# One copy in four of an attention's turned weights on VectorE instead of ScalarE, and one blank matmul fewer ahead of each pair of units

## The chip, the cores and the metric

The kernel runs on one core of a Trainium2 chip. The metric is the device time of one execution in microseconds (us), the median of several runs. The core has four compute engines that run side by side, each of them through its own instructions in order: TensorE (PE in the profile; its weight loads are PEld), VectorE (DVE), ScalarE (ACT) and GpSimd (POOL). They wait for one another through semaphores.

## The reference, cut to what matters

The reference chains six layers on an input of 2 x 16 x 16 x 64. The change touches the first, a neighbourhood attention with 8 heads over windows of 7 x 7:

```
attn = einsum('bijnd,bijnpqd->bijnpq', q, kn) + bias        # kn: the 7 x 7 window of keys
a = softmax(attn.reshape(B, H, W, NH, K * K), axis=-1)
out = einsum('bijnpq,bijnpqd->bijnd', a, vn).reshape(B, H, W, C)
out = out @ proj_w + proj_b
gate = sigmoid(relu(x @ g1_w + g1_b) @ g2_w + g2_b)
y = x + out * gate                                           # then a layer norm
```

After it come a global attention, a dilated attention, a mixture of experts, a causal attention over the batch, and a recurrence over 256 positions (`h_new = o * tanh(c_new)`), each of them with a norm ahead of it and each needing the whole of the one before.

## The kernel before, in words

The first attention is cut into 16 units (`NU`). A unit is one batch element, one half of the 256 positions (128 rows) and one pair of heads; the window is handled as 176 dense keys with a bias of -1e30 outside it. Two units make a pair `s` that shares one set of score matmuls. For a unit `u` the work goes round the engines:

1. TensorE, `scores(s)` (L436): 8 matmuls for both units of a pair, into two banks. It waits for the row minima of the pair before the last (`neg_max`), then issues two blank matmuls (`keep_clock`, L394) from the third pair on. A blank matmul multiplies a tile of zeros into a free bank; nobody reads it.
2. VectorE, `row_min(u)` (L753): adds the bias and takes the row minimum, once per head.
3. ScalarE, `numerators(u)` (L275): the exponentials of both heads with their sums.
4. VectorE, `normalise(u)` (L760 and L762): reciprocal of the sums, then a multiplication per head in place.
5. TensorE, `turn(u)` (L448): four transposes into bank 4 or 5, by the parity of `u`. It waits for `normalise(u)` and for the copy of unit `u - 2`, whose bank it takes.
6. ScalarE, `turned_copy(u)` (L283): copies that bank, 88 partitions by 512 columns, to one of four tiles `pt`.
7. TensorE, `values(s)` (L463): 16 matmuls for a pair, which read the copies of both of its units.

The loops fix the order on each engine by hand. TensorE at an even step `u` issues `scores(u/2)`, `turn(u-3)`, `values(u/2-3)`, and at an odd step `turn(u-3)` alone. ScalarE at step `u` issues `numerators(u)` and then `turned_copy(u-3)`. VectorE at step `u` issues `row_min(u)` and then `normalise(u-1)`, and at step 14 also `of0` (L776), the bias addition on the first half of the results. After the last `values`, ScalarE adds the bias to the second half (`of1`, L303), TensorE projects, and the rest of the program follows, all of it behind that point.

Of the kernel before, what the change touches and what calls it, by code (L numbers as in the profile page):

```python
# [27 lines left out]
KCH = KEYS // 2  # L28
# [45 lines left out]
def build(nc, x, const, later, vec, positions, w0, w1, w2, w3, w4, w5, out):  # L74
    with ExitStack() as ctx:
        def sb(name, shape, dt=F32):
            return ctx.enter_context(nc.sbuf_tensor(name, shape, dt))
# [3 lines left out]
        def on(name):  # L81

            if name not in semaphores:
                semaphores[name] = ctx.enter_context(nc.semaphore("s_" + name))
            return semaphores[name]

        bank = [ctx.enter_context(nc.psum_tensor(f"bank{i}", [P, 512], F32)) for i in range(8)]
# [14 lines left out]
        def v(name):  # L102
            return cols(vcs, VECS, name)
# [16 lines left out]
        pt = sb("pt", [KCH, 4, 4, P])  # L120
# [73 lines left out]
        NU = len(UNITS)  # L194
# [3 lines left out]

        block = ctx.enter_context(nc.Block())

        @block.sync
        def _(sp):
            for b in range(B):
                sp.dma_start(xtm[:, :, b], x[b].rearrange("(h p) c -> p h c", h=HALVES)).then_inc(on("x_in"), 16)
            sp.dma_start(cst[:], const).then_inc(on("const_in"), 16)
            for pair in range(HEADS // 2):
                sp.dma_start(rel[:, pair], positions[:, pair]).then_inc(on("rel_in%d" % pair), 16)
            for w, name, dram in ((ltr, "later_in", later), (w1s, "w1_in", w1), (w2s, "w2_in", w2), (w3s, "w3_in", w3),
                                  (w5s, "w5_in", w5), (w4s, "w4_in", w4)):
                sp.dma_start(w[:], dram).then_inc(on(name), 16)  # L210
            for h in range(HALVES):
                sp.wait_ge(on("y_tm"), h + 1)
                sp.dma_start(out[:, h * P:(h + 1) * P, :].rearrange("b p c -> p b c"), ytm[:, h]).then_inc(on("out"), 16)
            sp.wait_ge(on("out"), 16 * HALVES)
# [33 lines left out]
        def _(act):  # L248
# [20 lines left out]
            def numerators(u):  # L269
                act.wait_ge(on("neg_max"), 2 * u + 2)  # L270
                if u >= 5:
                    act.wait_ge(on("p_turned"), u - 4)
                for h in range(2):
                    k = 2 * u + h
                    act.activation(pr[:, u % 5, h], sc[:, u % 4, h], ACT.Exp, bias=nmx[:, k:k + 1], scale=-1.0,  # L275
                                   accum_out=sums[:, k:k + 1]).then_inc(on("p_ready"), 1)


            def turned_copy(u):
                act.wait_ge(on("p_turned"), u + 1)  # L280
                if u >= 4 and u % 2 == 0:
                    act.wait_ge(on("pv_mm"), u // 2 - 1)
                act.activation(pt[:, u % 4].rearrange("p a c -> p (a c)"), bank[4 + u % 2][0:KCH, :], ACT.Copy)\  # L283
                   .then_inc(on("pt_ready"), 1)

            for u in range(NU + 3):
                if u < NU:
                    numerators(u)
                if u == 1:
                    act.wait_ge(on("v0_mm"), 4)  # L290
                    act.wait_ge(on("vch_zero"), 1)
                    act.activation(vch[:, :, :, 0:HD].rearrange("p a h d -> p (a h) d"),
                                   bank[6][0:KCH, :].rearrange("p (a d) -> p a d", d=HD), ACT.Copy)\
                       .then_inc(on("vch"), 1)
                if u == 2:
                    act.wait_ge(on("g2_mm"), 1)
                    act.wait_ge(on("g2bh"), 1)
                    act.activation(gateh[:], bank[7][:, 0:N], ACT.Tanh, bias=g2bh[:], scale=0.5)\
                       .then_inc(on("gateh"), 1)
                if u >= 3:  # L300
                    turned_copy(u - 3)
            act.wait_ge(on("pv_mm"), NU // 2)
            act.activation(of[:, 1], bank[7][:], ACT.Identity, bias=v("bv0_1")).then_inc(on("of1"), 1)  # L303
# [83 lines left out]
        def _(pe):  # L387
            mm = pe.matmul

            def keep_clock(free_bank, n):  # L390


                for _ in range(n):
                    mm(free_bank[:], blank[:, 0:P], blank[:], start=True, stop=True, skip_group_check=True)  # L394
# [28 lines left out]
            def scores(s):  # L423

                b, qt, first = UNITS[2 * s]
                at = KROW0[qt] * SIDE
                if s >= 2:
                    pe.wait_ge(on("neg_max"), 4 * (s - 1))
                if s % PER_HALF == 0:
                    pe.wait_ge(on("km"), first + 2)  # L430
                if s >= 2:
                    keep_clock(bank[2 * (s % 2)], 2)
                for j in range(2):
                    for h in range(2):
                        r = slice((2 * b + h) * ROWS, (2 * b + h + 1) * ROWS)
                        m = mm(bank[2 * (s % 2) + h][:, j * KEYS:(j + 1) * KEYS], q0[r, qt * P:(qt + 1) * P],  # L436
                               km[r, first + j, at:at + KEYS], start=True, stop=True)
                m.then_inc(on("s_mm"), 1)

            def turn(u):  # L440
                pe.wait_ge(on("normalised"), u + 1)
                if u >= 2:
                    pe.wait_ge(on("pt_ready"), u - 1)
                if u == 1:
                    pe.wait_ge(on("k0"), 1)
                for h in range(2):
                    for ch in range(2):
                        m = pe.transpose(bank[4 + u % 2][0:KCH, (2 * h + ch) * P:(2 * h + ch + 1) * P],  # L448
                                         pr[:, u % 5, h, ch * KCH:(ch + 1) * KCH], ident)
                m.then_inc(on("p_turned"), 1)  # L450

            def values(s):

                pe.wait_ge(on("pt_ready"), 2 * s + 2)
                if s == 0:
                    pe.wait_ge(on("vch"), 1)
                for ch in range(2):
                    for u in (2 * s, 2 * s + 1):
                        b, qt, pair = UNITS[u]
                        g, j = divmod(pair, 2)  # L460
                        for h in range(2):
                            row = 32 * (2 * j + h)
                            m = mm(bank[6 + g][row:row + 32, (b * HALVES + qt) * P:(b * HALVES + qt + 1) * P],  # L463
                                   vch[:, 2 * qt + ch, b * HEADS + HEADS // 2 * h + pair], pt[:, u % 4, 2 * h + ch],
                                   start=(ch == 0), stop=(ch == 1), skip_group_check=True)
                m.then_inc(on("pv_mm"), 1)

            pe.wait_ge(on("q0"), 1)
            for u in range(NU + 4):
# [8 lines left out]
                if u >= 6 and u % 2 == 0:  # L478
                    values(u // 2 - 3)
            values(NU // 2 - 1)  # L480
            keep_clock(bank[4], 3)
            for g in range(2):
# [120 lines left out]
            for h in range(HALVES):  # L603
                for b in range(B):
                    u = h * B + b
# [28 lines left out]
            for h in range(HALVES):  # L634
                for b in range(B):
                    u, at = h * B + b, b * N + h * P
# [75 lines left out]
        def _(dve):  # L712
# [3 lines left out]
            def link(ins):  # L716

                links[0] += 1
                ins.then_inc(on("dve_link"), 1)
                dve.wait_ge(on("dve_link"), links[0])  # L720
# [7 lines left out]
            def masked_k(h):  # L728

                head = c("heads")[:, h:h + 1]  # L730
                if h < 2:
                    m = ts(km[:, h], bank[5][:, 0:N], v("bk0"), head, ALU.add, ALU.mult)
                else:
                    m = ts(km[:, h], k0[:], head, None, ALU.mult)
                m.then_inc(on("km"), 1)
# [21 lines left out]
            def normalise(u):  # L757
                k = 2 * u
                dve.wait_ge(on("p_ready"), k + 2)
                link(dve.reciprocal(rsum[:, k:k + 2], sums[:, k:k + 2]))  # L760
                for h in range(2):
                    m = ts(pr[:, u % 5, h], pr[:, u % 5, h], rsum[:, k + h:k + h + 1], None, ALU.mult)  # L762
                m.then_inc(on("normalised"), 1)

            for u in range(NU + 1):
                if u < NU:
                    row_min(u)
                if u >= 1:
                    normalise(u - 1)
                if u in (2, 4):  # L770
                    if u == 2:
                        dve.wait_ge(on("k0"), 1)
                    masked_k(2 + u // 4)
                if u == NU - 2:
                    dve.wait_ge(on("pv_mm"), NU // 4)
                    ts(of[:, 0], bank[6][:], v("bv0_0"), None, ALU.add).then_inc(on("of0"), 1)  # L776
# [70 lines left out]
            for d in range(3):  # L847
                dve.wait_ge(on("k2_ready"), d + 1)
                dve.wait_ge(on("qkv2_mm"), 2 * d + 2)
                for j in range(3):  # L850
                    s = PADT + (j - 1) * DIL[d]
# [244 lines left out]
```

## Time and profile before

| | |
|---|---|
| three runs | 415.60, 415.72, 413.05 us; median 415.6 |
| the profiled execution | 415.62 us, of which its span in the profile is 413.8 us (1.8 us lie around the span) |
| first attention, first scores to last `values` | 8.6 to 35.6 us |
| the following layers | to about 111 us |
| the recurrence | about 111 us to the end |

All times of a row are microseconds from the start of the span, unless marked ns. A start is when the instruction begins to execute, and the second number is its duration. Two instructions in a row on one engine overlap a little, so that the distance from one start to the next is what an instruction costs its engine. The granted clock is a share of TensorE's 2.4 GHz: 1.00 is 2.4, 0.50 is 1.2 GHz.

### The profile page before, as it was taken

The numbers are of one execution on the slowest core, as the hardware profiler recorded it, in microseconds if no ns is written. First come the engines' busy times: TensorE is split into PE (matmuls) and PEld (weight loads), VectorE is DVE, ScalarE is ACT, GpSimd is POOL, SyncE is SP. The second block draws the span as 40 slices with busy tenths as digits, with TensorE's granted clock in tenths as the row PEclk, the third lists the DMA queues.
The fourth block names the chain that finished last, engine by engine and source line by source line (L and its number), as shares of the span: only waits on it lengthen the run. The fifth ranks groups of instructions, "written<-read, shape, count | busy, mean of one in ns | idle before, by whom it ended". The sixth has DMA issues, their size and how long they took to land.

```text
span 413.8 us, 11957 instructions
## 1 busy us (share of the span) xinstructions
PE 287.3 (69%) x3339; PEld 221.6 (54%) x3348; DVE 254.9 (62%) x2299; ACT 211.1 (51%) x1172; POOL 11.5 (3%) x21
## 2 busy tenths in 40 slices
PE   8898899899866666556666666556666666656663
PEld 3564458533555555555555555555555555555553
DVE  2884634554366666666666666666666666666665
ACT  2995434164555555555555555555555555555552
POOL 4006000000000000000000000000000000000000
PEclk9999996999955555555555555555555555555555
DMA  7600000000000000000000000000000000000000
GB/s 270 247 2 0 2 0 2 0 0 2 1 2 1 0 0 0 0 0 0 0 0 0 0 0 0 0 0 0 0 0 0 0 0 0 0 0 0 0 0 13
DMA packets 2972, 5.60 MB, mean 14 GB/s; under 512 B 1424, under 2 KB 1680, under 8 KB 2960
## 3 DMA queue, kind: packets, MB, share of 16 engines
q1 hardware_dynamic: 2672, 5.09, 3.4%
q10 hardware_dynamic: 288, 0.36, 0.3%
q8 instruction: 6, 0.10, 0.1%
q14 instruction: 6, 0.05, 0.0%
HBM read 5.32 MB, written 0.13 MB: 13 GB/s over the span
## 4 chain that ended last, share of the span: by engine, by line
ACT 36%; PE 36%; DVE 16%; issue 11%; DVEq 0%; POOL 0%; POOLq 0%
ACT bank L383 19%; PE bank L681 16%; ACT gi L371 10%; DVE ha L965 6%; DVE terms_a L965 4%; ACT bank L373 4%; PE bank L394 3%; PE bank L448 1%; PE bank L613 1%; PE bank L436 1%; PE bank L574 1%; PE bank L625 1%; PE bank L496 1%; PE bank L511 1%; PE bank L502 1%
## 5 line engine op out<-in xcount | busy, mean ns | idle before, releaser
L681 PE MATMUL bank<-ha,vparts 128*128 128x1 f16 x1536 | 96.4, 169 | 111.0 <-DVE ha L965 111.0
L681 PEld LDWEIGHTS bank<-ha,vparts 128*128 128x128 f16 x1536 | 75.6, 107 | 133.7 <-DVE ha L965 133.7
L371 ACT ACTIVATE gi<-bank 128x1 f32<-128x1 f32 x256 | 43.8, 171 | 146.2 <-PE bank L681 146.2
L383 ACT ACTIVATE bank<-bank,hc,gi 128x2 f32<-128x2 f32 x256 | 83.3, 325 | 0.0
L962 DVE TENSOR_SCALAR go<-go 128x1 f32<-128x1 f32 x256 | 39.4, 154 | 68.1 <-ACT go L377 68.1
L681 PE MATMUL bank<-hb,vparts 128*128 128x1 f16 x768 | 77.4, 166 | 0.0
L681 PEld LDWEIGHTS bank<-hb,vparts 128*128 128x128 f16 x768 | 61.0, 104 | 0.0
L965 DVE CUSTOM_DVE_ANT_0 terms_a<-bank,go 128x3 f32<-128x3 f32 x256 | 41.3, 161 | 28.1 <-ACT bank L383 0.2
L677 PE MATMUL bank<-x,w5s 128*128 (+1 forms) x198 | 55.9, 358 | 0.0
L491 PE MATMUL bank<-ones,w5s 128*128 128x8 f32 x198 | 55.6, 355 | 0.0
L971 DVE SCALAR_TENSOR_TENSOR cell<-bank,gi,hc 128x1 f32<-128x1 f32 x256 | 54.8, 214 | 0.0
L677 PEld LDWEIGHTS bank<-x,w5s 128*128 128x128 f32 x198 | 49.0, 308 | 0.5 <-DVE x L801 0.5
L491 PEld LDWEIGHTS bank<-ones,w5s 128*128 128x128 f32 x198 | 48.8, 305 | 0.1
L377 ACT ACTIVATE go<-bank 128x3 f32<-128x3 f32 x256 | 48.3, 189 | 0.1
L975 DVE TENSOR_TENSOR hc<-hs,cell 128x1 f32<-128x1 f32 x256 | 40.9, 160 | 8.8
L373 ACT ACTIVATE bank<-bank 128x1 f32<-128x1 f32 x256 | 42.7, 167 | 0.0
L968 DVE CUSTOM_DVE_ANT_0 terms_b<-bank,go 128x4 f32<-128x4 f32 x256 | 40.2, 157 | 0.0
L973 DVE TENSOR_TENSOR hs<-bank,go 128x1 f32 x256 | 38.1, 149 | 0.0
L394 PE MATMUL bank<-blank 128*128 128x512 bf16 x81 | 25.5, 416 | 2.4 <-POOL blank L220 1.4
L965 DVE DVE_READ_ACCUMULATOR2_ANT ha<- 128x1 f16 x256 | 21.9, 86 | 0.0
L968 DVE DVE_READ_ACCUMULATOR2_ANT hb<- 128x1 f16 x256 | 21.8, 85 | 0.0
L275 ACT ACTIVATE pr<-sc,nmx 128x176 f32<-128x176 f32 x32 | 13.8, 432 | 2.4 <-DVE nmx L753 2.3
(212 smaller groups left out, 275.5 us busy)
## 6 DMA issues: line engine op xcount, KB each, us to landing
rel<-in_positions SPq DMA_DIRECT2D x4, 352.0 KB, 5.6
w3s<-in_w SPq DMA_DIRECT2D x1, 804.0 KB, 9.6
ltr<-in_later SPq DMA_DIRECT2D x1, 709.0 KB, 7.6
w2s<-in_w SPq DMA_DIRECT2D x1, 640.0 KB, 8.3
w5s<-in_w SPq DMA_DIRECT2D x1, 576.0 KB, 10.6
w0s<-in_w ACTq DMA_DIRECT2D x1, 336.0 KB, 3.8
w1s<-in_w SPq DMA_DIRECT2D x1, 256.0 KB, 7.6
w4s<-in_w SPq DMA_DIRECT2D x1, 192.0 KB, 10.6
```

Of the source, the lines that this page charges most:

```text
L371: act.activation(gi[:], bank[pre + 1][:, at:at + 1], ACT.Sigmoid, scale=1.0 / PRE)
L373: act.activation(gt, bank[pre][:, at:at + 1], ACT.Tanh, scale=1.0 / PRE)\
L377: act.activation(go[:, two, 0:3], bank[pre + 2][:, at:at + 1].broadcast_to([P, 3]), ACT.Sigmoid, scale=1.0 / PRE).then_inc(on("o_gate"), 1)
L383: act.activation(tc_ends, gt.broadcast_to([P, 2]), ACT.Tanh, scale=gi[:], bias=hc[:]).then_inc(on("tanh_c"), 1)
L491: return mm(bank[3 * parity + k][:, 0:CHUNK], w5s[:, (6 + k) * P:(7 + k) * P], ones[:], start=True, stop=False, skip_group_check=True)
L677: return mm(bank[3 * parity + k][:, 0:CHUNK], w5s[:, k * P:(k + 1) * P], x5[:, bass.ds(start, CHUNK)], start=False, stop=False, skip_group ...
L681: return mm(bank[3 * parity + k][:, at:at + 1], vparts[:, part, k], h, start=False, stop=False, skip_group_check=True)
L962: ts(go[:, two, 3:4], o, -1.0, None, ALU.mult).then_inc(on("minus_o"), 1)
L965: dve.tensor_tensor_reduce(terms_a[:, two], tq[:, 0:3], go[:, two, 0:3], HSCALE, 0.0, ALU.mult, ALU.add, ha[:]).then_inc(on("ha_ready"), 1)
L968: dve.tensor_tensor_reduce(terms_b[:, two], tq, go[:, two], -HSCALE, 0.0, ALU.mult, ALU.add, hb[:]).then_inc(on("hb_ready"), 1)
L971: stt(out=cell[:], in0=gt, scalar=gi[:], in1=hc[:], op0=ALU.mult, op1=ALU.add)\
L975: tt(hc[:], hs[:, bass.ds(t, 1)], cell[:], ALU.mult).then_inc(on("hc_ready"), 1)
```

## The change

VectorE does `turned_copy` for the units 3, 7, 11 and 15, at its steps 5, 9, 13 and 17, after `normalise` of that step; ScalarE leaves these four out. The semaphore `pt_ready` becomes two, one for each engine, and TensorE waits for the right count of both. The blank matmuls ahead of `scores` go from two to one; there are six such places, the pairs 2 to 7.

```
+        def copied(engine, n):
+            engine.wait_ge(on("pt_act"), n - n // 4)
+            if n // 4:
+                engine.wait_ge(on("pt_dve"), n // 4)
...
@@ ScalarE @@
                 act.activation(pt[:, u % 4].rearrange("p a c -> p (a c)"), bank[4 + u % 2][0:KCH, :], ACT.Copy)\
-                   .then_inc(on("pt_ready"), 1)
+                   .then_inc(on("pt_act"), 1)
...
-                if u >= 3:
+                if u >= 3 and u % 4 != 2:
                     turned_copy(u - 3)
...
@@ TensorE @@
                 if s >= 2:
-                    keep_clock(bank[2 * (s % 2)], 2)
+                    keep_clock(bank[2 * (s % 2)], 1)
...
             def turn(u):
                 pe.wait_ge(on("normalised"), u + 1)
                 if u >= 2:
-                    pe.wait_ge(on("pt_ready"), u - 1)
+                    copied(pe, u - 1)
...
             def values(s):
-                pe.wait_ge(on("pt_ready"), 2 * s + 2)
+                copied(pe, 2 * s + 2)
...
@@ VectorE @@
-            for u in range(NU + 1):
+            def turned_copy(u):
+                dve.wait_ge(on("p_turned"), u + 1)
+                if u >= 4:
+                    dve.wait_ge(on("pv_mm"), (u - 3) // 2)
+                dve.tensor_copy(pt[:, u % 4].rearrange("p a c -> p (a c)"), bank[4 + u % 2][0:KCH, :])\
+                   .then_inc(on("pt_dve"), 1)
+
+            for u in range(NU + 2):
                 if u < NU:
                     row_min(u)
-                if u >= 1:
+                if 1 <= u <= NU:
                     normalise(u - 1)
+                if u >= 2 and u % 4 == 1:
+                    turned_copy(u - 2)
```

## Rows read from the trace of the kernel before

**Rows 1.** The page: busy time by engine, then the chain that ended last.

```profile
PE 287.3 (69%) x3339; PEld 221.6 (54%) x3348; DVE 254.9 (62%) x2299; ACT 211.1 (51%) x1172; POOL 11.5 (3%) x21
...
ACT 36%; PE 36%; DVE 16%; issue 11%; DVEq 0%; POOL 0%; POOLq 0%
```

**Rows 2.** Windows by stage: busy us (instructions) by engine, then granted clock, DMA share, GB/s.

```profile
10.00:35.60 25.60, 22.32 (x264) 14.82 (x267) 20.45 (x114) 23.22 (x82) 4.26 (x5) 1.00 0.26 106
35.60:65.15 29.55, 26.50 (x152) 15.59 (x155) 14.19 (x44) 12.73 (x28) 2.54 (x4) 1.00 0.00 1
65.15:72.00 6.85, 6.63 (x23) 5.38 (x25) 3.22 (x12) 2.87 (x6) 0.00 (x0) 0.51 0.01 2
...
112.90:413.80 300.90, 186.04 (x2669) 162.91 (x2668) 194.62 (x2043) 151.72 (x1018) 0.00 (x0) 0.50 0.00 1
```

**Rows 3.** Timeline of TensorE, one pair: start, duration, instruction.

```profile
25.25 0.87 PE L436 MATMUL bank<-km,q 32*128 32x176 f32 x8
26.05 0.64 PE L448 MATMUL bank<-cst,pr 128*88 128x128 f32 x4
26.62 0.64 PE L463 MATMUL bank<-pt,vch 88*32 88x128 f32 x16
27.20 0.64 PE L448 MATMUL bank<-cst,pr 128*88 128x128 f32 x4
27.67 0.59 PE L394 MATMUL bank<-blank 128*128 128x512 bf16 x2
28.20 0.87 PE L436 MATMUL bank<-km,q 32*128 32x176 f32 x8
28.99 0.64 PE L448 MATMUL bank<-cst,pr 128*88 128x128 f32 x4
```

**Rows 4.** Timeline of ScalarE, one unit: numerators, then a copy.

```profile
26.81 0.44 ACT L275 ACTIVATE pr<-sc,nmx 128x176 f32<-128x176 f32 x1 [0.17 <-DVE nmx L753]
...
27.68 0.58 ACT L283 ACTIVATE pt<-bank 88x512 f32<-88x512 f32 x1
```

**Rows 5.** Timeline of VectorE, one unit: row minimum, reciprocal, normalisation.

```profile
26.17 0.34 DVE L753 CUSTOM_DVE_ANT_0 sc<-bank,rel 128x176 f32<-128x176 f32 x1 [0.52 <-PE bank L436]
...
26.70 0.16 DVE L760 RECIPROCAL rsum<-sums 128x2 f32<-128x2 f32 x1
26.89 0.53 DVE L762 TENSOR_SCALAR pr<-pr,rsum 128x176 f32<-128x176 f32 x2
27.34 0.33 DVE L753 CUSTOM_DVE_ANT_0 sc<-bank,rel 128x176 f32<-128x176 f32 x1
```

**Rows 6.** Instructions on the `pt` tiles: duration ns min/median/max.

```profile
L283 ACT ACTIVATE pt<-bank x16: 574/577/593, 14.7 to 34.3; 88x512 f32<-88x512 f32 x16
...
L838 DVE COPY pt<-bank x1: 684/684/684, 51.5 to 51.5; 128x512 f32<-128x512 f32 x1
```

**Rows 7.** Timeline of TensorE, early: `turn(2)`, then `turn(3)`.

```profile
15.46 0.61 PE L448 MATMUL bank<-cst,pr 128*88 128x128 f32 x4 [1.07 <-ACT pt L283]
...
17.23 0.64 PE L448 MATMUL bank<-cst,pr 128*88 128x128 f32 x4
```

**Rows 8.** Timeline of the end of the stage, all engines.

```profile
30.28 0.74 DVE L776 TENSOR_SCALAR of<-bank,vcs 128x512 f32<-128x512 f32 x1
...
31.32 1.03 POOL L232 CAST oneh<-ltr 24x1024 bf16<-24x1024 f32 x1
...
31.65 1.03 DVE L762 TENSOR_SCALAR pr<-pr,rsum 128x176 f32<-128x176 f32 x2
...
32.44 1.05 ACT L283 ACTIVATE pt<-bank 88x512 f32<-88x512 f32 x2
...
33.16 1.09 PE L448 MATMUL bank<-cst,pr 128*88 128x128 f32 x8 [0.64 <-ACT pt L283]
...
33.80 1.08 ACT L283 ACTIVATE pt<-bank 88x512 f32<-88x512 f32 x2 [0.31 <-PE bank L448]
```

**Rows 9.** The chain of waits, its last step in the stage.

```profile
34.94 0.65 PE bank L463 x16
```

## The prediction

> **What bounds the kernel now.** I read the page first, then windows by stage, then the timelines of the engines inside the one stage that the change touches. The page gives no engine more than 69% of the span, and its chain of waits passes from ScalarE to TensorE to VectorE [rows 1]: a program of stages that hand work on. The windows say how much is at stake. From 112.9 us to the end, 300.9 us of the 413.8, runs the recurrence, which the diff leaves alone [rows 2]. The first attention takes about 27 us, 6.5% of the time. Whatever the change does must happen there, and what follows moves with it one for one, since the projection waits for the last `values`.
>
> Inside the stage the timeline of TensorE has no hole for a whole pair: scores at 25.25, a turn at 26.05, values at 26.62, a turn at 27.20, two blanks at 27.67, the next scores at 28.20 [rows 3]. That is 2.95 us a pair, made of 0.80 + 0.57 + 0.58 + 0.57 + 0.43, where the last is what is left of 1.00 for a turn and two blanks, so 0.21 for one blank. VectorE in the same pair sat idle for 0.52 and ScalarE for 0.17 [rows 4, 5]. So TensorE bounds the middle of the stage, by work of which 0.43 is blank, with ScalarE close behind. The reader is to see that both halves of the change aim at this balance.
>
> **What is removed.** One blank less is 0.21 us, in six places: 1.3 us at most. Of these the one ahead of the third pair is lost, because `turn(2)` right behind it sat 1.07 us waiting for ScalarE's first copy, which does not move [rows 7]. On ScalarE a copy costs 0.48 (two take 1.05 where one takes 0.577, [rows 6, 8]), so four take 1.9 us of work off it. Per two pairs ScalarE then holds 4 x 0.86 + 3 x 0.48 = 4.9 us (0.86 from numerators to copy, [rows 4]).
>
> **What is added.** VectorE gets four copies from PSUM. The nearest row is its copy of 128 x 512 with 684 ns [rows 6]; this one has the same 512 columns in fewer partitions, and ScalarE's copies of 88 and of 128 partitions need nearly the same, so I take 0.68. A successor starts some 0.08 before the recorded end (26.89 + 0.53 against 27.34, [rows 5]), so the copy holds VectorE for 0.60. From below I bound it by ScalarE's 0.48, from above by the 0.74 of VectorE's addition on 128 x 512 [rows 8]. A unit holds VectorE for 1.17 us, 0.53 for the minima and 0.64 for the normalisation [rows 5], so two pairs with a copy need 5.3 us, and TensorE with one blank 5.5, where now they take 5.9. By sums of busy time alone the change fits, and would gain.
>
> **Where the copy stands.** The order decides. At its step 9 VectorE has finished `row_min(9)` and `normalise(8)`, and now waits for `turn(7)`. But TensorE issues `turn(7)` only behind `scores(5)`. Before, VectorE took that very moment to start `row_min(10)` on these scores: it starts 0.92 us after they do (25.25 to 26.17, [rows 3, 5]), whereas a copy can start only 0.80 + 0.64 after them, 0.64 being the step from a turn to its copy (33.16 to 33.80, [rows 8]). So `row_min(10)` starts 0.52 + 0.60 = 1.1 us later. Queued behind the waiting copy are `row_min(10)`, `normalise(9)`, `row_min(11)`, `normalise(10)`; ScalarE waits for those minima, with its own copies queued behind its exponentials; TensorE waits for those copies. Followed round, this closes a loop over two pairs, from one VectorE copy to the next:
>
> copy 0.60; `row_min(10)` 0.53; `normalise(9)` 0.64; `row_min(11)` until ScalarE can start 0.64 (26.17 to 26.81, [rows 4, 5]); `numerators(11)` 0.86; ScalarE's copy of unit 8 until TensorE can start 0.72 (32.44 to 33.16, [rows 8]); `turn(10)` 0.57; one blank 0.21; `scores(7)` 0.80; `turn(11)` until its copy starts 0.64. Sum: 6.21 us.
>
> That is longer than the 5.9 of two pairs before, with the gain of the blanks already in it. From `turn(3)` to `turn(11)` there are two such loops, 12.42 us against 28.99 - 17.23 = 11.76 [rows 3, 7]: 0.66 more. `turn(3)` itself comes 0.21 earlier (the blank ahead of the fourth pair). Net 0.45 later at `turn(11)`.
>
> **The end of the stage.** Here `of0` stands in VectorE's order between `normalise(13)` and `row_min(15)`, and the last copy is VectorE's own. From `turn(11)`: 0.64 to the copy; copy 0.60; `row_min(14)` 0.53; `normalise(13)` 0.64; `of0` 0.66 (0.74 less the 0.08); `row_min(15)` 0.64; `numerators(15)` 0.86; copy of 12 to `turn(14)` 0.72; `turn(14)` 0.57; `turn(15)` to its copy 0.64; VectorE's copy of 15, 0.68 and a handover of 0.05 as from ScalarE's last copy to 34.94 [rows 8, 9]: 7.23 us. Before it took 34.94 - 28.99 = 5.95 [rows 3, 9]. So 1.28 more.
>
> **The sum.** 0.45 + 1.28 = 1.7 us later at the last `values`. Behind it nothing takes this up: ScalarE's `of1`, the projection and each further stage wait for it, and no transfer is late (the DMA share is 0.00 from 35.6 on, [rows 2]). The profiled execution took 415.62 us, almost the median of 415.6; 415.6 + 1.7 = 417.3 us.
>
> Two costs stay outside the sum. A GpSimd cast ran from 31.32 for 1.03 us, and the normalisation beside it took 1.03 instead of 0.53 [rows 8]; GpSimd starts behind `of0`, so it moves along, and may now fall on `normalise(14)`, which has some 0.9 us of slack, or on the last copy, for up to 0.5 more. And splitting a semaphore adds a wait instruction to TensorE's turns and values: I price it at nothing, as it is met before its turn comes, up to 0.1 at the seams.
>
> **The rivals.** First, that the copy costs VectorE no more than its idle 0.52 per pair, so that TensorE stays the bound and the blanks come off as paid. This would be so if VectorE's wait did not hold back what stands behind it, or if `turn(7)` came ahead of VectorE's need. For it: VectorE idles 1.0 us per two pairs and needs 0.6. Against it: that idle time lies ahead of `row_min(10)`, while `turn(7)` follows the scores. It gives 5 x 0.21 = 1.1 us less, 414.5. The Trainium skill, in "TensorEngine Tiling (Array Packing)", PSUM Bottleneck, advises the same: to use both ScalarE and VectorE for emptying PSUM. By that advice the time is this rival's; no row of before shows the two sharing these copies.
>
> Second, that TensorE's clock falls. It did fall once ahead of the recurrence, from 65.15 to about 72 us, to 0.51, after a run of tiny matmuls, and came back [rows 2]; the first attention has 1.00 throughout. The new waits leave TensorE idle for some 0.8 us ahead of `turn(13)` and 1.6 ahead of `turn(14)`, where the longest idle there now is 0.64 [rows 8]. If a fall begins there and lasts the same 6.85 us, it costs at most half of that, 3.4 us: 420.7 us, slower by 1.2%. It decides only if the clock falls before about 36 us. Against it: TensorE sat 1.07 us idle at 15.46 with the clock kept [rows 2, 7]. The page "TensorE: Matmul & The Clock Gate", Part 1, of the Trainium skill says that activity releases the throttle and idleness brings it back; the trace agrees in kind, but shows no fall from holes of this size.
>
> Third, that the fall at 65 us does not come. It costs at most the same 3.4 us, and one of the three runs was 2.6 us shorter, 413.05, which I take, without proof, for a run without it. A stage that ends 1.7 us later shifts everything under that clock. If most runs after are of this kind: 417.3 - 2.6 = 414.7. This would not be the work of the edit's copies.
>
> **How the numbers follow.** The forecast, a stage longer by 1.0 to 2.5 us, has a chance of 0.60: 0.48 for the copy takes 0.5 off over its four places, 0.74 adds up to 0.4, and the cast another 0.5, so 416.7 to 418.2. The copy hidden: 0.14. The clock falling in the stage: 0.06. The fall at 65 us missing in the median: 0.20. The range must take in the first, second and last of these, 414.1 to 418.5. What a measurement of this kernel can tell from no change is 1%, 4.2 us. Slower by more needs the fallen clock, 0.05; faster by more needs hidden copies and no fall together, 411.9, and a little beyond, 0.02; the rest is within.
>
> **What the profile after would show.** VectorE idle ahead of each of its four `pt` copies, released by TensorE's turn, about 0.7 to 1.1 us; `row_min(6)`, `(10)`, `(14)` right behind them; ScalarE waiting about 1.0 us for the minima of units 6, 10 and 14; TensorE waiting for ScalarE's copies 0.75 us ahead of `turn(6)` and `turn(10)`; from one VectorE copy to the next 6.2 us; the last `values` starting at about 36.7. I am wrong if TensorE still has no hole between 19 and 30 us and a pair takes 2.73, if the stage is late but the end is not, or if the clock row shows another pattern than before.

## The result and the profile after

The changed kernel took 416.18 us (median of 20 runs, 414.65 to 419.02), the kernel before 413.84 (20 runs, 412.65 to 416.26, the three shown at first among them). The ratio is 1.0065, with a 95% interval of 1.0047 to 1.0083: slower by 2.3 us, inside the 1% that was called no change. The forecast was 417.3, from a base of 415.6.

The stage can be timed in every profile on its own, from the first scores to the start of ScalarE's `of1` (L303, now L309). The two ends before, then after:

```profile
8.63 0.86 PE L436 MATMUL bank<-km,q 32*128 32x176 f32 x8 [0.20 <-DVE km L732]
...
35.65 0.69 ACT L303 ACTIVATE of<-bank,vcs 128x512 f32<-128x512 f32 x1 [0.76 <-PE bank L463]
```

```profile
8.60 0.86 PE L442 MATMUL bank<-km,q 32*128 32x176 f32 x8 [0.20 <-DVE km L738]
...
38.51 0.69 ACT L309 ACTIVATE of<-bank,vcs 128x512 f32<-128x512 f32 x1 [2.23 <-PE bank L469]
```

Before, that is 35.65 - 8.63 = 27.02 us; after, in this execution, 38.51 - 8.60 = 29.91.

The page of the changed kernel, busy time and granted clock in tenths over 40 slices of 10.4 us:

```profile
PE 289.4 (69%) x3342; PEld 221.5 (53%) x3342; DVE 256.9 (62%) x2303; ACT 209.4 (50%) x1168; POOL 11.6 (3%) x21
...
PEclk9996997899975555555555555555555555555555
```

ScalarE has 1.7 us less and VectorE 2.0 us more work than in [rows 1]; in the clock row there are two dips ahead of the recurrence, the fourth and the seventh to eighth slice. The profiled execution took 419.02 us, the longest of the twenty. Its windows, cut where the clock changes:

```profile
8.60:34.32 25.72, 20.45 (x232) 13.80 (x232) 21.90 (x118) 20.34 (x77) 1.65 (x3) 1.00 0.31 126
34.32:41.16 6.84, 6.56 (x51) 3.68 (x51) 1.42 (x4) 3.43 (x6) 5.23 (x6) 0.50 0.00 0
...
68.46:75.28 6.82, 6.82 (x25) 5.35 (x25) 2.55 (x10) 2.32 (x5) 0.00 (x0) 0.50 0.01 2
...
119.66:417.20 297.54, 183.91 (x2646) 160.93 (x2646) 193.25 (x2026) 150.35 (x1008) 0.00 (x0) 0.50 0.00 1
```

The dip at 68.46 is that of [rows 2] at 65. The one from 34.32 to 41.16 is new, and it begins in the first attention. VectorE's timeline:

```profile
17.66 0.69 DVE L775 COPY pt<-bank 88x512 f32<-88x512 f32 x1 [0.61 <-PE bank L454]
18.27 0.33 DVE L759 CUSTOM_DVE_ANT_0 sc<-bank,rel 128x176 f32<-128x176 f32 x1
...
23.83 0.69 DVE L775 COPY pt<-bank 88x512 f32<-88x512 f32 x1 [0.71 <-PE bank L454]
24.43 0.33 DVE L759 CUSTOM_DVE_ANT_0 sc<-bank,rel 128x176 f32<-128x176 f32 x1
...
30.00 0.69 DVE L775 COPY pt<-bank 88x512 f32<-88x512 f32 x1 [0.71 <-PE bank L454]
...
33.13 1.03 DVE L768 TENSOR_SCALAR pr<-pr,rsum 128x176 f32<-128x176 f32 x2
...
36.54 0.69 DVE L775 COPY pt<-bank 88x512 f32<-88x512 f32 x1 [1.69 <-PE bank L454]
```

The first three copies start 6.17 us apart, the last one 6.54 behind the third; each sits behind a wait for TensorE's turn (L454), and a row minimum (L759) stands right behind the first three. ScalarE in the same stretch:

```profile
25.07 0.44 ACT L281 ACTIVATE pr<-sc,nmx 128x176 f32<-128x176 f32 x1 [0.90 <-DVE nmx L759]
...
27.09 0.58 ACT L289 ACTIVATE pt<-bank 88x512 f32<-88x512 f32 x1
...
33.92 1.05 ACT L289 ACTIVATE pt<-bank 88x512 f32<-88x512 f32 x2
```

It waits 0.90 us for the minima of unit 10 and copies unit 8 only at 27.09. TensorE waits for that:

```profile
26.45 0.64 PE L469 MATMUL bank<-pt,vch 88*32 88x128 f32 x16
27.77 0.61 PE L454 MATMUL bank<-cst,pr 128*88 128x128 f32 x4 [0.68 <-issue]
28.22 0.38 PE L400 MATMUL bank<-blank 128*128 128x512 bf16 x1
28.52 0.86 PE L442 MATMUL bank<-km,q 32*128 32x176 f32 x8
29.32 0.64 PE L454 MATMUL bank<-cst,pr 128*88 128x128 f32 x4
...
31.90 0.64 PE L454 MATMUL bank<-cst,pr 128*88 128x128 f32 x4 [0.80 <-DVE pr L768]
...
34.60 1.90 PE L454 MATMUL bank<-cst,pr 128*88 128x128 f32 x8 [1.48 <-DVE pr L768]
```

Where [rows 3] had no hole for a pair, there is now one of 0.68 ahead of `turn(10)`, 0.80 ahead of `turn(13)` and 1.48 ahead of `turn(14)`. For the last the profile names VectorE's normalisation, which ended at 33.13 + 1.03 = 34.16; ScalarE's copy of unit 12 from 33.92 to about 34.5 came later and is what TensorE waited for. The two last turns take 1.90 us at the low clock where they took 1.09 at the full one [rows 8].

### The profile page after: what moved, and what is told of

Read it like the earlier page. It is cut to its first block, busy times and chain, and to the rows that moved or that the text cites. A ratio compares the mean times of both kernels' runs of the same rounds, so it can differ in the third digit from the quotient of the medians.

```text
span 417.2 us, 11964 instructions
## 1 busy us (share of the span) xinstructions
PE 289.4 (69%) x3342; PEld 221.5 (53%) x3342; DVE 256.9 (62%) x2303; ACT 209.4 (50%) x1168; POOL 11.6 (3%) x21
## 4 chain that ended last, share of the span: by engine, by line
PE 37%; ACT 37%; DVE 15%; issue 10%; POOL 0%; DVEq 0%; POOLq 0%
ACT bank L389 21%; PE bank L687 17%; ACT gi L377 11%; DVE ha L980 6%; DVE terms_a L980 4%; ACT bank L379 4%; PE bank L400 3%; PE bank L454 2%; PE bank L580 1%; PE bank L619 1%; PE bank L442 1%; PE bank L631 1%; PE bank L469 1%; PE bank L502 1%; PE bank L517 1%
## 5 line engine op out<-in xcount | busy, mean ns | idle before, releaser
L687 PE MATMUL bank<-hb,vparts 128*128 128x1 f16 x768 | 76.4, 165 | 0.0
L400 PE MATMUL bank<-blank 128*128 128x512 bf16 x84 | 27.1, 427 | 1.4 <-POOL blank L226 1.4
## 6 DMA issues: line engine op xcount, KB each, us to landing
w4s<-in_w SPq DMA_DIRECT2D x1, 192.0 KB, 10.4
```

The source lines that it names most:

```text
L687: return mm(bank[3 * parity + k][:, at:at + 1], vparts[:, part, k], h, start=False, stop=False, skip_group_check=True)
```

## The experiments

Two things had to be told apart: the order on VectorE (a stage longer by what the loop says), and TensorE's clock. "Stage" below is the time from the first scores to `of1` in the profile of each kernel, and its forecast is the one written down before that kernel ran, all of it for a clock that is kept. All ratios are to the kernel before on the same chip.

| kernel | stage, us | against 27.02 | forecast by the order | median, us (runs) | ratio, 95% interval |
|---|---|---|---|---|---|
| changed, first profile | 29.91 | +2.89 | +1.7 | 416.18 (20) | 1.0065, 1.0047 to 1.0083 |
| copies only, two blanks | 29.32 | +2.30 | +2.2 | 416.14 (12) | 1.0042, 1.0020 to 1.0065 |
| one blank only | 25.95 | -1.07 | -1.1 | 413.27 (12) | 0.9973, 0.9950 to 0.9996 |
| copies behind the minima | 27.09 | +0.07 | 0.0 | 414.75 (12) | 1.0007, 0.9986 to 1.0028 |
| wait only | 27.19 | +0.17 | +0.1 | 415.87 (13) | 1.0025, 1.0009 to 1.0041 |
| changed again | 29.10 | +2.08 | +1.6 | 416.18 (12) | 1.0046, 1.0021 to 1.0072 |
| end holes filled | 28.67 | +1.65 | +1.6 | 414.66 (12) | 1.0002, 0.9983 to 1.0020 |
| other holes filled | 29.02 | +2.00 | +1.6 to 1.7 | 417.59 (9) | 1.0068, 1.0040 to 1.0097 |
| changed, `of0` late | 28.00 | +0.98 | +1.0 | 414.96 (12) | 1.0011, 0.9994 to 1.0029 |
| all on ScalarE, one blank, `of0` late | 25.44, 25.44 | -1.58 | -1.55 | 412.49 (12), 412.89 (12) | 0.9968, 0.9944 to 0.9993; 0.9967, 0.9949 to 0.9985 |
| units 4, 8, 12, `of0` late | 25.37, 25.36 | -1.65 | -1.6 | 411.96 (8), 411.35 (7) | 0.9938, 0.9910 to 0.9965; 0.9936, 0.9913 to 0.9959 |

The three rows that miss the order's forecast by more than 0.1, the two of the changed kernel and the one with other holes filled, are those whose profile has the clock at 0.50 ahead of `of1`.

### Either part alone

```
-                    keep_clock(bank[2 * (s % 2)], 1)
+                    keep_clock(bank[2 * (s % 2)], 2)          # in the changed kernel
```

> The changed kernel with two blank matmuls ahead of each pair again: VectorE's four copies alone. By the order theory (VectorE waits for a turn that stands behind the scores, and the row minima wait behind the copy) the loop over two pairs takes 6.21 + 0.21 = 6.4 us and the last values end some 2.2 us later than before, about 0.6 us later than in the changed kernel. If instead the missing blanks made the loss (by the clock), this one is at or below the time of before, with no low clock ahead of 60 us.

The copies, on VectorE:

```profile
17.38 0.69 DVE L775 COPY pt<-bank 88x512 f32<-88x512 f32 x1 [0.83 <-PE bank L454]
...
23.77 0.69 DVE L775 COPY pt<-bank 88x512 f32<-88x512 f32 x1 [0.93 <-PE bank L454]
```

They are 6.39 us apart, 0.22 more than with one blank: the blank is part of the loop. The clock was 1.00 until 66.9 in this profile, so a stage 2.30 us longer is the copies' doing. The holes at the end are there as in the changed kernel, 0.80 ahead of `turn(13)` and then:

```profile
34.75 1.10 PE L454 MATMUL bank<-cst,pr 128*88 128x128 f32 x8 [1.48 <-DVE pr L768]
```

So this execution had both holes and kept its clock. Two of its 12 runs took 418.55 and 418.58, as eight of the changed kernel's 20 took over 417.3; that the clock fell in those is not shown.

```
-                    keep_clock(bank[2 * (s % 2)], 2)
+                    keep_clock(bank[2 * (s % 2)], 1)          # in the kernel before
```

> The kernel before with one blank matmul instead of two ahead of each pair, all copies on ScalarE. By the order theory the stage ends 1.1 us earlier than before, ScalarE being the bound of the middle at 2.66 us a pair. If the missing blanks cost clock, some executions show a clock of 0.5 ahead of 45 us and are up to 3 us longer. If the blanks were hidden anyway, the time is that of before.

Stage 1.07 us shorter, no run of 12 above 414.39. The blanks come off as paid, and nothing shows that taking them away brings the clock down by itself. In the stage the change is a gain of 1.1 and a loss that outweighs it.

### The place of the copy

```
-            for u in range(NU + 2):
+            for u in range(NU + 3):
                 if u < NU:
                     row_min(u)
+                if u >= 3 and u % 4 == 2:
+                    turned_copy(u - 3)
...
-                if u >= 2 and u % 4 == 1:
-                    turned_copy(u - 2)
```

> The changed kernel with each VectorE copy one step later in VectorE's order, between row_min of the next unit and normalise (steps 6, 10, 14 and 18). By the order theory the wait for the turn is then covered by the row minima and the stage ends about as before (35.7 us, 1.6 us earlier than the changed kernel). By the rival that VectorE simply has too much work, or that its copy from PSUM is what costs, it stays within 0.4 us of the changed kernel.

```profile
22.70 0.69 DVE L775 COPY pt<-bank 88x512 f32<-88x512 f32 x1
23.31 0.15 DVE L766 RECIPROCAL rsum<-sums 128x2 f32<-128x2 f32 x1
...
28.34 0.69 DVE L775 COPY pt<-bank 88x512 f32<-88x512 f32 x1
...
30.96 1.02 DVE L768 TENSOR_SCALAR pr<-pr,rsum 128x176 f32<-128x176 f32 x2
...
33.54 0.69 DVE L775 COPY pt<-bank 88x512 f32<-88x512 f32 x1 [0.87 <-PE bank L454]
```

The same four copies, 0.69 us each, the first three with no wait ahead of them (the fourth waits 0.87 for its turn): 5.64 apart instead of 6.17, and a stage as long as before. The place of the copies alone makes 28.67 - 27.09 = 1.58 us, with 28.67 for the changed kernel with its clock kept (measured below). But they are not free here: with one blank and no VectorE copies the stage is 25.95, 1.14 shorter. The row at 30.96 is again a normalisation that takes 1.02 instead of 0.53.

```
                 if u >= 1:
                     normalise(u - 1)
+                if u >= 2 and u % 4 == 1:
+                    dve.wait_ge(on("p_turned"), u - 1)          # kernel before, one blank
```

> The kernel before with one blank matmul ahead of each pair and, on VectorE, only the wait for the turn of units 3, 7, 11 and 15 at the places where the changed kernel has its copies; the copies are ScalarE's. By the order theory the wait alone costs 1.1 us against the same kernel without it (stage end about 35.8, so the time of before), the copy's own 0.6 us the rest. By the rival that the copy's duration is the whole cost, this one takes the time of the kernel with one blank.

```profile
22.89 0.34 DVE L753 CUSTOM_DVE_ANT_0 sc<-bank,rel 128x176 f32<-128x176 f32 x1 [0.76 <-PE bank L448]
```

The row minimum now waits for the turn (L448) instead of the scores. The stage is 27.19, 1.24 longer than with one blank and no such wait. So of the 28.67 - 25.95 = 2.72 us between one blank alone and the changed kernel with its clock kept, a wait without any copy makes 1.24 and the copies the other 1.48. The 0.6 that I had written down for the copies was wrong by my own loop, which holds the copy's 0.60 once per copy. The median of this kernel, 415.87, is higher than its stage accounts for: 11 of its 13 runs lie between 415.79 and 415.98, while the profiled one took 413.87 with the dip behind 65 us only 3.4 us long instead of 6.8. The stage's length is not in doubt, and the length of that dip is worth a step of about this size (the end of the experiments shows it), but why so many of its runs are in the upper group is open.

### The clock

The changed kernel once more:

> The changed kernel once more. If the granted clock stays at 1.00 in the first attention, the order theory expects 28.6 us from the first scores to ScalarE's of1 (27.0 before, plus 1.6), with VectorE's copies 6.2 us apart; with the clock fallen ahead of turn(14), as in its first profile, 29.9 us. If the loss were all clock, a profile with the clock kept would show 27.0 or less.

```profile
8.10:35.94 27.84, 21.67 (x253) 14.93 (x256) 23.14 (x121) 21.59 (x79) 3.69 (x4) 1.00 0.30 124
35.94:39.36 3.42, 2.97 (x22) 1.48 (x25) 0.17 (x1) 2.13 (x3) 3.10 (x5) 0.50 0.00 0
```

This execution took 417.34 us; the clock fell later, at 35.94, just ahead of the last `values`, and for half as long. Copies again 6.17 apart. No profile of the changed kernel itself shows the clock kept; that expectation was answered only by the next kernel.

```
             def turn(u):
+                if u in (13, 14):
+                    keep_clock(bank[0], 3 if u == 13 else 6)
                 pe.wait_ge(on("normalised"), u + 1)
```

> The changed kernel with three more blank matmuls ahead of turn(13) and six ahead of turn(14), where TensorE only waits (0.8 and 1.6 us). By the clock theory these holes are what lets the clock fall in the stage in some executions, so the group of runs some 3 us above the others goes, and the highest run lies at about 417. By the rival that the fall comes with the rest of the stage, or is chance, that group stays. The stage itself is as long as in the changed kernel with the clock kept, 28.6 us.

```profile
30.30 0.81 PE L400 MATMUL bank<-blank 128*128 128x512 bf16 x3
31.27 0.64 PE L456 MATMUL bank<-cst,pr 128*88 128x128 f32 x4 [0.15 <-DVE pr L770]
...
32.64 1.24 PE L400 MATMUL bank<-blank 128*128 128x512 bf16 x5 [0.16 <-issue]
33.96 1.10 PE L456 MATMUL bank<-cst,pr 128*88 128x128 f32 x8
```

Clock 1.00 through the stage (one of the nine blanks has no record), and the stage 28.67 us, 1.65 longer than before: the order's share, measured with the clock kept. The slowest of 12 runs took 415.86. The changed kernel had 11 of 32 runs above 417.3 in two sets, and none of this one is. Its median is 1.5 us lower, but that is more than the missing group accounts for: the nine of the 12 runs of the changed kernel beside it that lie below 417.3 have a median of 415.93, still 1.3 above 414.66. Nine of the 12 runs with filled holes lie between 414.4 and 414.8 and the profiled one, at 415.74, has the later dip 6.8 us long; a shorter later dip in the others would make such a step, and whether the blanks have anything to do with it is not shown.

```
                 pe.wait_ge(on("normalised"), u + 1)
+                if u in (6, 10):
+                    keep_clock(bank[2], 3)
```

> Control for the filled holes: the changed kernel with three more blank matmuls ahead of turn(6) and of turn(10) each, in the 0.7 us that TensorE waits there, and none ahead of turn(13) and turn(14). If the fall of the clock comes from the two holes at the end of the stage, the group of runs at 418.5 to 419 stays and the median is that of the changed kernel, 416.2. If any more TensorE work in the stage keeps the clock, this one behaves as the kernel with those holes filled, 414.7 and none above 417. The stage is as long as in the changed kernel with the clock kept, up to 0.1 more.

Six blanks filled in elsewhere do not take the group away: 5 of 9 runs at 417.6 to 418.8, and the profile again has the clock fallen, from 36.18 to 39.60. It is the emptiness at the end of the stage that matters. One of its holes alone was not seen to do it: the kernel with the copies behind the minima has 0.28 ahead of `turn(13)` and the same 1.48 ahead of `turn(14)`, clock 1.00 in its profile, and no run of 12 above 415.67.

```profile
29.72 0.64 PE L454 MATMUL bank<-cst,pr 128*88 128x128 f32 x4 [0.28 <-DVE pr L768]
...
32.42 1.09 PE L454 MATMUL bank<-cst,pr 128*88 128x128 f32 x8 [1.48 <-DVE pr L768]
```

### The end of the stage

```
-                if u == NU - 2:
+                if u == NU:
                     dve.wait_ge(on("pv_mm"), NU // 4)
                     ts(of[:, 0], bank[6][:], v("bv0_0"), None, ALU.add).then_inc(on("of0"), 1)
```

> The changed kernel with of0 moved from step 14 to step 16 on VectorE, nothing else. The order theory has of0 (0.66 us) as one term of the end of the stage, between normalise(13) and row_min(15): the last values 0.66 us earlier than in the changed kernel with the clock kept, so a stage of about 28.0 us, and the hole ahead of turn(14) 0.66 shorter, so fewer falls of the clock there and fewer runs at 418 to 419. If of0 is not on the path, the stage stays at 28.6.

```profile
31.44 0.64 PE L454 MATMUL bank<-cst,pr 128*88 128x128 f32 x4 [0.80 <-DVE pr L768]
...
33.48 1.09 PE L454 MATMUL bank<-cst,pr 128*88 128x128 f32 x8 [0.82 <-issue]
```

The hole ahead of `turn(14)` shrank from 1.48 to 0.82, the stage to 28.00, by 0.67 against the 0.66 of the term, and no run of 12 is above 415.23. One addition moved by two steps takes back about half of the loss in the median, which is 1.2 us above that of before instead of 2.3.

The same move in the kernel before with one blank, all copies on ScalarE:

> The kernel before with one blank matmul ahead of each pair and VectorE's addition of0 moved from step 14 to step 16, behind all normalisations; all copies on ScalarE. By the order theory 0.5 us more than the missing blanks bring, the last values 1.55 us earlier than before, since nothing then stands between the row minima and normalise(13) to (15). If the end of the stage hangs on something else, it equals the kernel with one blank, 1.07 us earlier than before.

And VectorE's copies at places where nobody waits for them, units 4, 8 and 12, with the counts in `copied` and the waits for `pv_mm` to match:

```
+                if u - 3 in (4, 8, 12):
+                    turned_copy(u - 3)          # between row_min(u) and normalise(u - 1)
...
-                if u == NU - 2:
+                if u == NU:
```

> VectorE copies units 4, 8 and 12 only, each behind row_min of unit u + 3, when its turn is long done; of0 at step 16; one blank. By the order theory VectorE never waits for its copy and the stage ends 1.6 us earlier than before, as early as with all copies on ScalarE and of0 moved: the copy taken off ScalarE brings nothing once nobody waits for it. By the rival that ScalarE is the bound once a blank is gone, it ends 0.3 us or more earlier than the kernel with of0 moved alone.

```profile
18.13 0.69 DVE L775 COPY pt<-bank 88x512 f32<-88x512 f32 x1
...
23.58 0.69 DVE L775 COPY pt<-bank 88x512 f32<-88x512 f32 x1
```

Copies without a wait, 5.45 apart, which is two pairs of TensorE with one blank each. Both stages are 1.6 us shorter than before, and both medians are below either of the case; by stage the copies on VectorE bring 0.07. Each was run again:

> Again: all copies on ScalarE, one blank, of0 at step 16. Stage of 25.4 us; a median of 412.5 within 0.5, to be set beside the next kernel on the same chip.

> Again: VectorE copies units 4, 8 and 12 behind the row minima, of0 at step 16, one blank. Stage of 25.4 us; by the order theory the same time as the kernel before it within 0.5 us, since both stages are as long. If the copies off ScalarE bring something the stage does not show, it is faster by more than 0.5 us again.

The medians differ by 0.5 and then by 1.5 us, in favour of the copies on VectorE, where the stage differs by 0.08. A part of it is seen behind the stage. The addition that makes `y0`, all on ScalarE, then with units 4, 8 and 12 on VectorE:

```profile
36.24 0.75 DVE L783 TENSOR_TENSOR y<-pg,xf 128x256 f32<-128x256 f32 x1
```

```profile
35.56 0.42 DVE L798 TENSOR_TENSOR y<-pg,xf 128x256 f32<-128x256 f32 x1
```

The first began 0.03 us after a GpSimd instruction (L239, at 36.21). The second began 0.20 us ahead of that instruction (L245 there, at 35.76), which then took 1.25 us instead of 1.17. The second pair of profiles shows 0.76 and 0.42 again. That is 0.33 us, which hangs on which of the two starts first.

More lies in the recurrence, whose code is the same in both. `terms_a` is a VectorE instruction of each of its 256 steps. From the first to the last of them pass 297.14 us with all copies on ScalarE and 296.61 with the three on VectorE. Over all profiles it is 296.96 to 297.22 in the five profiles without a `pt` copy of this stage on VectorE and 296.36 to 296.61 in the nine profiles with some. Half of the 0.53 is one step, 0.27 us longer in the first, where one instruction waits longer for its ScalarE result. First without and then with the copies on VectorE:

```profile
127.81 0.15 DVE L962 TENSOR_SCALAR go<-go 128x1 f32<-128x1 f32 x1 [0.75 <-ACT go L377]
```

```profile
126.97 0.15 DVE L977 TENSOR_SCALAR go<-go 128x1 f32<-128x1 f32 x1 [0.39 <-ACT go L383]
```

Why is open. With 0.08 in the stage, 0.33 in `y0`, 0.53 in the recurrence, and 0.07 and 0.12 at the two ends, the 1.13 us between the two later profiles are all placed; the 1.5 between the medians are not.

The same kernels profiled twice also show what the later dip is worth. All copies on ScalarE: no dip ahead of the recurrence in one profile and 3.4 us of it in the other, and from `of1` to the first `terms_a` 73.97 and 74.95 us. Units 4, 8 and 12 on VectorE: a dip of 6.8 and of 3.4 us, and 76.24 and 74.62 us. So which of them an execution draws moves its time by 1 to 1.6 us each, and a median of 7 or 8 runs can move by it.

## Why the prediction was right, point by point

**TensorE the bound, blanks as paid.** Right: the stage is 1.07 us shorter with one blank instead of two, for 5 x 0.21.

**The copy's duration.** Taken as 0.68, measured 0.69; it holds VectorE 0.60 to 0.61 (23.83 to 24.43).

**The loop of two pairs.** Forecast 6.21, measured 6.17; with two blanks 6.42 and 6.39. The rival that held the copy for hidden is refuted in this order, and holds in another: placed behind the row minima the copies cost 1.1 us in the stage instead of 2.7, and three of them, on units 4, 8 and 12 and with `of0` late, nothing.

**The end of the stage.** The two holes were forecast at 0.8 and 1.6 and are 0.80 and 1.48. `of0` as a term of 0.66 on the path was confirmed by moving it.

**The sum.** 1.7 us longer with the clock kept; measured 1.65 in the kernel with its end holes filled. The band beside it, 1.0 to 2.5, is not quite what its own terms give, 1.2 to 2.6; nothing hangs on that. The slowed normalisation that I left outside the sum did fall on `normalise(14)` (33.13, 1.03 us) and cost nothing, having slack, as said.

**What follows moves one for one.** This step did not hold, and the prediction had no term for it. In the profile with the end holes filled, beside that of before and with the later dip 6.8 us long in both, the stage is 1.65 longer, but from `of1` to the first `terms_a` pass 75.94 us instead of 76.46 and through the recurrence 296.48 instead of 297.05. From the first scores to the end it is only 0.5 us longer. The copies alone with two blanks, the same way: 2.30 in the stage, 1.4 in all. The recurrence is shorter by about 0.6 in every profile with copies on VectorE; the cause is open.

**What was mis-sized.** The second rival, the fall of TensorE's clock in the stage. Its place was right, the holes ahead of `turn(13)` and `turn(14)`, but it had a chance of 0.06 and was treated as a case for all runs or none. It is an event of single executions: 11 of 32 runs of the changed kernel lie above 417.3, the two profiled among them took 419.02 and 417.34 with low stretches of 6.84 and 3.42 us, and with the holes filled no run is up there. Against the profile with the holes filled, from the first scores to the end, these two are 3.0 and 1.8 us longer, where the prediction had at most 3.4. In how many of the other runs the clock fell is not known. The prediction had also said that it was wrong if the clock row showed another pattern than before: by that sign of its own it was, in both profiles of the changed kernel. My argument against it, that a hole of 1.07 us at 15.46 left the clock alone, compared one hole; here TensorE has two of them within 3.5 us, with 1.2 us of work between. The same two holes were there in the profile of the copies with two blanks, and the clock stayed.

**The base.** The 415.6 from which I counted was the upper of at least two groups of the kernel before, between 412.6 and 414 and, seven of 20 runs, between 415.4 and 416.3; with 20 runs the median is 413.84. So 417.3 is 1.1 too high though the difference of 1.7 was too small against 2.3. The two errors have opposite signs. That 417.3 came within 1.1 us is in part luck: a base too high, a stage rightly forecast, some 1 us given back behind it, and in some executions a fall of the clock that took 1.8 to 3.0. How much of the 2.3 is the order and how much the clock cannot be cut cleanly: the kernel with the holes filled has the full 1.65 in its stage and is only 0.8 above the median of before (ratio 1.0002). No experiment held the later dip fixed, so how often each kernel draws the long one, and what that does to its median, is argued, not shown.

## What to carry to other kernels

Work moved to an engine with idle time is free only if its input is there when its turn comes: look at what releases that engine's idle time, and put the piece behind an instruction that is ready earlier, not where the count of steps would have it. Follow the loop of waits over one full period before trusting sums of busy time; here it gave each stage to 0.1 us wherever the clock was kept. It did not give the time of the whole kernel: measure what follows the stage too, since it need not move one for one. And where the clock can fall, see how long the new holes are taken together, and compare groups of runs rather than one median.

## What the runs showed of the hardware

- The same kernel on the same data had TensorE's clock fall inside the first attention in both profiled executions, for 3.4 and 6.8 us; the same two holes in the kernel with two blanks left it at 1.00. The fall came at 34.32, inside the second hole, in one and at 35.94, 1.8 us after that hole had ended, in the other, where TensorE had been busy for 1.81 of the 4.0 us from 30 to 34 at a full clock. With blank matmuls in these holes it stayed at 1.00; with 1.48 us of hole alone it did too.
- A low stretch ahead of the recurrence was absent in one profile, 3.4 us long in four and 6.8 us in nine; in two pairs of profiles of one kernel each, 3.4 us more of it went with 1.0 and 1.6 us more time.
- VectorE's multiplication on SBUF took 1.03 instead of 0.53 us for two beside a GpSimd cast, and `y0` 0.75 instead of 0.42 where GpSimd had started first. VectorE's copies out of PSUM took 0.686 to 0.689 us in all four places, one of them, at 36.54, beside a GpSimd instruction.
- A piece of code that no edit touched, the recurrence, took 0.3 to 0.9 us less in every profile with `pt` copies of the first attention on VectorE; one of its waits was 0.39 instead of 0.75 us.
